# Splitting the weights inside the first pass, and a product moved from DVE to Pool

## The chip, the cores and the metric

One core of a Trainium2 chip (trn2) runs the whole program in one launch. Time is device time in microseconds. Engines: TensorE (PE, with its weight loads PEld), VectorE (DVE), ScalarE (ACT), GpSimd (POOL), SyncE (SP, here only an issuer of DMAs). Each has its own instruction queue, in order; they wait for each other by semaphores.

## The reference

x is (16, 512, 256) in float32. Two layers with residuals: an attention-like mixer, then a mixture of experts. Cut to what matters:

```python
# mixer, on LN(x)
xx = shift of the first 64 channels forward, of the next 64 back by one token
xk, xv, xr = x*mix + xx*(1 - mix)            # one mix per k, v, r
k, v, r = xk @ Wk.T, xv @ Wv.T, xr @ Wr.T
# scan over tokens, per channel, ew = exp(decay/T), u = first/T
out = (a + exp(u + k)*v) / (b + exp(u + k))
a, b = a*ew + exp(k)*v, b*ew + exp(k)
x1 = x + LN((sigmoid(r) * out) @ Wo.T)
# mixture of experts, on LN(x1): 8 experts, the best 2 by softmax(logits)
y = sum over the 2 of gate_e * expert_e(x1n) + shared(x1n)    # each silu(w1 x)*(w3 x) @ w2
out = x1 + LN(y)
```

## The kernel before

Every float32 matrix product is made of three products of parts: each operand is a `hi` (rounded by ACT) plus a `lo` (operand minus hi, by DVE or POOL), and PE adds hi*hi, hi*lo, lo*hi. So the weights have to be split once, and every activation as it comes.

Three stages follow each other: `first_pass` (mixer, routing, shared expert), `expert_tiles`, `combine`. The change is in the first alone. Its sequences s = 0 to 15 of 512 tokens go through a software pipeline, written out by hand as one `body(i)` for each engine. In body i the work on k, v, r and the scans is for sequence i (`kvr`, `exps`, `scans`, `denominator`, `invert`, `gate`), that on the output projection and x1 for i-1 (`project`, `normalise_o`, `add_x`), routing and the inner part of the shared expert for i-2 (`route`, `count_tokens`, `inner`), its outer part for i-3 (`outer`, `read_y`). Bodies 3 to 15 hold all of these. The order inside a body is the order in which calls stand there, on each engine by itself; nothing reorders them.

Ahead of that, `split_weights` is a block of its own with a barrier at its end: it loads the weights, mixes them into three parts for the channels as they are (HERE), shifted (SHIFT) and the other 128 (REST), and splits all. Only then does the pass begin, and it waits for all 15 constants.

What the prediction's steps touch:
- PE, `kvr` L537, `project` L561, `count_tokens` L602, `inner` L613, `outer` L630. The second half of `outer` waits for `y_read`, since both halves use one PSUM bank.
- ACT, in body order: h_high(3), f_high(0), high_w, exps(0), f_high(1), gate_exp, exps(1), silu(0), normalise_o (tile `on`), g_high(0) (tile `g_hi`, L721), read_y(0) (L782), silu(1), normalise_x (tile `xn`), and so on to g_high(1).
- DVE: the scans b_sum L866 and a_sum L869, reciprocals L886, `gate` L894 (g = num * den), f_low L910, the copy of token numbers L940, `low_w` L1012. `low_w` makes the lo part of one sixteenth of the expert weights in each body; SP stores both parts to `w_split` for the second stage.
- POOL: `running_sums` (num L1129, den L1131), add_x L1147, g_low L1137, h_low L1153, the scales of the normalisations L50 to L55, and `send` L1161, indirect DMAs that scatter rows to the experts' slots.

## Time and profile before

| | us |
|---|---|
| median of 3 runs (1188.23 to 1189.91) | 1188.67 |
| the profiled execution | 1182.5 |
| its span | 1180.7 |
| PE busy | 1001.1 (85%) |
| DVE busy | 880.2 (75%) |
| POOL busy | 771.6 (65%) |
| ACT busy | 568.9 (48%) |

The busy share is a mean over three stages with different limits. The first 31 us have almost no PE work; from there to about 650 the first pass runs, and then the experts. The profile shows the time of each instruction and, in brackets, how long its engine sat idle before it and what ended that. Times of instructions in the steady bodies repeat from body to body to 0.1 us or so, so one body can be read as all.

### The profile page before, as it was taken

To read this page: it belongs to the slowest core of one execution; us is meant where nothing else is said; L and a number is where in the kernel's file an instruction comes from. 1 tells how busy PE (TensorE), PEld (TensorE's weight loads), DVE (VectorE), ACT (ScalarE), POOL (GpSimd) and SP (SyncE) were. 2 spreads that over 40 slices of the span, in tenths; PEclk is the share of its full clock that TensorE was granted. 3 is DMA by queue.
4 is the path that set the end of the run, shared out by engine and by line. 5 is a ranking of instruction groups with operands and counts; after the bars stand their busy time and mean duration, and the time that the engine had idled before them with its cause. 6 is when DMAs were issued, how large, how long until landed. Compare 5 with 4: busy or idle time off the path is not lost. (4 is left out here: it accounts for less than half of the span.)

```text
span 1180.7 us, 23300 instructions
## 1 busy us (share of the span) xinstructions
PE 1001.1 (85%) x6344; PEld 886.1 (75%) x6344; DVE 880.2 (75%) x2211; ACT 568.9 (48%) x1013; POOL 771.6 (65%) x790
## 2 busy tenths in 40 slices
PE   0668899999999999999997875889999999999452
PEld 0457688788878887888786764889999999999341
DVE  3588888988898889888988323656777767777486
ACT  3344564556455645564555233434444444444265
POOL 2234876787678767876786444256776667666598
PEclk9878999999999999999999777889999999999655
DMA  4233432453235323532441117679768788887797
GB/s 136 76 107 99 147 116 88 130 165 112 88 129 165 114 87 129 165 115 85 131 148 55 59 50 229 193 174 223 125 112 183 144 204 162 184 200 183 191 371 324
DMA packets 109813, 174.06 MB, mean 147 GB/s; under 512 B 13741, under 2 KB 77896, under 8 KB 109512
## 3 DMA queue, kind: packets, MB, share of 16 engines
q1 hardware_dynamic: 78568, 121.09, 31.5%
q0 software_dynamic: 26592, 35.67, 16.7%
q10 hardware_dynamic: 4608, 16.78, 3.8%
q8 instruction: 19, 0.31, 0.1%
q14 instruction: 26, 0.21, 0.1%
HBM read 173.53 MB, written 78.21 MB: 213 GB/s over the span
## 5 line engine op out<-in xcount | busy, mean ns | idle before, releaser
L1511 POOL DMA_INDIRECT sum_y<-e_y,e_row_at x142 | 224.2, 1579 | 42.8 <-issue 38.7
L1343 PE MATMUL e_h_ps<-e_z_hi,e_w 128*128 128x256 f32 x1136 | 218.9, 285 | 11.2 <-DMA e_w<-w_split 6.3
L1343 PEld LDWEIGHTS e_h_ps<-e_z_hi,e_w 128*128 128x128 f32 x1136 | 182.4, 192 | 15.0 <-issue 8.6
L1161 POOL DMA_INDIRECT slots_x<-f_xf,f_at x128 | 143.8, 1123 | 37.8 <-issue 37.8
L1343 PE MATMUL e_h_ps<-e_z_lo,e_w 128*128 128x256 f32 x568 | 160.6, 283 | 0.0
L1387 ACT ACTIVATE e_act_h<-e_h_ps,e_w 128x256 f32<-128x256 f32 x142 | 67.4, 475 | 182.9 <-PE e_h_ps L1343 167.8
L1359 PE MATMUL e_y_ps<-e_w,e_h_hi 128*128 128x256 f32 x568 | 118.3, 292 | 1.1 <-DVE e_h_lo L1433 1.1
L625 PE MATMUL f_h_ps<-f_f_hi,f_w_hi 128*128 128x512 f32 x256 | 107.5, 420 | 6.7 <-ACT f_act_h L766 3.9
L886 DVE RECIPROCAL f_den<-f_den 128x256 f32<-128x256 f32 (+1 forms) x48 | 109.2, 2278 | 0.6
L1343 PEld LDWEIGHTS e_h_ps<-e_z_lo,e_w 128*128 128x128 f32 x568 | 108.5, 191 | 0.0
L1426 DVE SCALAR_TENSOR_TENSOR e_h<-e_h_ps,e_w,e_act_h 128x256 f32<-128x256 f32 x142 | 67.3, 482 | 52.5 <-ACT e_act_h L1387 51.0
L625 PE MATMUL f_h_ps<-f_f_hi,f_w_lo 128*128 128x512 f32 x256 | 102.8, 402 | 0.0
L625 PE MATMUL f_h_ps<-f_f_lo,f_w_hi 128*128 128x512 f32 x256 | 102.6, 401 | 0.0
L919 DVE SCALAR_TENSOR_TENSOR f_h<-f_h_ps,f_bias,f_act_h 128x512 f32<-128x512 f32 x64 | 47.8, 747 | 63.0 <-ACT f_act_h L766 60.7
L1359 PEld LDWEIGHTS e_y_ps<-e_w,e_h_hi 128*128 128x128 f32 x568 | 92.2, 188 | 1.3 <-DVE e_h_lo L1433 1.3
L1129 POOL TENSOR_TENSOR f_num<-f_num,f_a_sum 128x512 f32<-128x512 f32 x32 | 41.3, 1292 | 77.1 <-DVE f_a_sum L869 76.8
L1153 POOL TENSOR_TENSOR f_h_lo<-f_h,f_h_hi 128x512 fp32r<-128x512 f32 x64 | 81.9, 1293 | 13.4 <-ACT f_h_hi L774 12.7
L1147 POOL TENSOR_TENSOR f_x<-f_on,f_x_res 128x1024 f32<-128x1024 f32 x16 | 38.8, 2424 | 73.4 <-ACT f_on L727 73.4
L34 POOL TENSOR_TENSOR e_scratch<-e_scratch 128x1 f32<-128x1 f32 x71 | 27.3, 384 | 87.2 <-DMA sum_y<-e_y,e_row_at 40.1
L766 ACT ACTIVATE f_act_h<-f_h_ps,f_bias 128x512 f32<-128x512 f32 x64 | 43.8, 685 | 82.1 <-PE f_h_ps L625 82.1
L1359 PE MATMUL e_y_ps<-e_w,e_h_lo 128*128 128x256 f32 x284 | 79.8, 281 | 0.0
L645 PE MATMUL f_shared_ps<-f_w_hi,f_h_hi 128*128 128x256 f32 x256 | 73.7, 288 | 4.8 <-POOL f_h_lo L1153 4.2
(222 smaller groups left out, 2988.9 us busy)
## 6 DMA issues: line engine op xcount, KB each, us to landing
e_w<-w_split SPq DMA_DIRECT2D x71, 514.0 KB
e_w<-w_split SPq DMA_DIRECT2D x71, 512.0 KB
...
```

The costliest lines, as they stand in the source:

```text
L625: last = pe.matmul(out[:, :], a[:, which, c, q * P:(q + 1) * P], b[p][:, c, :], start=(n == 0), stop=(n == 5))
L645: last = pe.matmul(y_ps[:, j, :], a[:, q, at:at + P], b[:, q, :], start=(n == 0), stop=(n == 3 * Q - 1))
L766: act.activation(act_h[q % 2][:, :], h1_ps[:, :], ACT.Silu, bias=bias[:, 0, q:q + 1])\
L886: dve.reciprocal(den[c][:, at], den[c][:, at]).then_inc(rec_ready, 1)
L919: dve.scalar_tensor_tensor(out=h[q][:, :], in0=h3_ps[:, :], scalar=bias[:, 1, q:q + 1], in1=act_h[q % 2][:, :], op0=ALU.add, op1=ALU.mult) ...
L1153: pool.tensor_tensor(h_lo[:, q, :], h[q][:, :], h_hi[:, q, :].bitcast(F32), ALU.subtract)\
L1161: pool.indirect_dma_start(out=slots_x[:, :], out_offset=bass.IndirectOffsetOnAxis(ap=at[p][:, j, k:k + 1], axis=0), in_=xf[p][:, j, :], in ...
L1343: last = pe.matmul(h_ps[q][:, which, :], w13(p, q, part)[:, which, c, :], z[p % 2][:, c, :], start=(n == 0), stop=(n == 5))
L1359: last = pe.matmul(y_ps[p % 2][:, j, :], a[p % 2][:, q, j * P:(j + 1) * P], w2(p, part)[:, q, :], start=(n == 0), stop=(n == 3 * parts - 1))
L1387: act.activation(act_h[q][:, :], h_ps[q][:, 0, :], ACT.Silu, bias=bias(p, 0, q)).then_inc(silu_ready, 1)
L1426: dve.scalar_tensor_tensor(out=h[p % 2][:, q, :], in0=h_ps[q][:, 1, :], scalar=bias(p, 1, q), in1=act_h[q][:, :], op0=ALU.add, op1=ALU.mul ...
L1511: pool.indirect_dma_start(out=dst[:, :], out_offset=bass.IndirectOffsetOnAxis(ap=row_at[p][:, j:j + 1], axis=0), in_=y[p][:, j, :], in_off ...
```

## The change

Three things. (1) `split_weights` is gone as a block: its steps stand at the beginning of each engine's program in `first_pass`, in another order, with x of sequence 0 loaded before the attention weights; the buffers of the raw weights lie in rooms used later for something else; the waits for split weights are put before the first product that needs each. ACT issues three constants itself. (2) Moves inside the body: `high_w` behind f_high(1) on ACT, `low_w` from behind the moments of x to behind the aggregate of x1 on DVE, the stores of `w_split` to behind the load of x on SP, the copy of the token numbers from DVE to ACT; a small addition of one element stands in its place on DVE. (3) `gate` goes from DVE to POOL: g(0) behind add_x, g(1) between two sends.

```diff
-        split_weights(nc, attn_w, mix, ffn_w, gate_w, w_hi, w_lo, wo_hi, wo_lo, w13, w2, gw, load_ahead)
+        w_all = x1_room[:, :, :, :].rearrange("p a b n -> p (a b n)").rearrange("p (w c n) -> p w c n", w=4, c=CC)
+        w_mixed = exps_room[:, :, :].rearrange("p a n -> p (a n)")[:, 0:9 * C].rearrange("p (w a n) -> p w a n", w=3, a=3)
+        ffn_raw = h_room[:, :, :].rearrange("p a n -> p (a n)")
         @block.sync
         def _(sp):
+            sp.dma_start(mix_c, mix).then_inc(mix_in, 16)
+            sp.dma_start(x_in[0][:, :, :], by_tiles(x[0, :, :])).then_inc(x_loaded[0], 16)
+            sp.dma_start(w_all, attn_w).then_inc(w_in, 16)
+            sp.dma_start(ffn_raw, ffn_w).then_inc(ffn_in, 16)
+            sp.dma_start(gw_raw, gate_w).then_inc(ffn_in, 16)
+            sp.dma_start(x_in[1][:, :, :], by_tiles(x[1, :, :])).then_inc(x_loaded[1], 16)
...
         @block.tensor
-            pe.wait_ge(consts_in, 16 * CONSTS)
+            pe.wait_ge(first_consts_in, 16 * 3)
...
+                    if isinstance(s, int) and s == 0:
+                        pe.wait_ge(wlo_ready, (HERE, REST, SHIFT).index(part) + 1)
...
         @block.scalar
+            act.dma_start(decay_c[:, :], decay).then_inc(first_consts_in, 16)
+            act.dma_start(first_c[:, :], first).then_inc(first_consts_in, 16)
+            act.dma_start(eye[:, :], ident).then_inc(first_consts_in, 16)
...
                 normalise(LN_X1, s, p, xf[p], x1[p]).then_inc(xf_ready, 1)
+                act.activation(xf[p][:, :, C], number_s[:, bass.ds(s * SUBS, SUBS)], ACT.Copy).then_inc(numbered, 1)
...
                 f_high(i - 2, par, 0)
-                high_w(i)
                 exps(i, 0)
                 f_high(i - 2, par, 1)
+                high_w(i)
                 gate_exp(i - 2)
...
+            high_part(HERE)
+            normalise_x(0, 0)
+            high_part(REST)
+            high(0)
+            high_part(SHIFT)
+            act.activation(wo_hi[:, :, :], w_all[:, 3, :, :], ACT.Copy).then_inc(wo_hi_ready, 1)
+            act.wait_ge(ffn_in, 32)
+            act.activation(flat(w13["hi"][:, :, :, :]), ffn_raw[:, 0:W13_COLS], ACT.Copy).then_inc(ffn_hi_ready, 1)
...
         @block.vector
-                wait(dve, sent[p], landed(s - 2, p, 2 * SUBS))
-                dve.tensor_copy(xf[p][:, :, C], number_s[:, bass.ds(s * SUBS, SUBS)]).then_inc(numbered, 1)
+                dve.tensor_tensor(shift[:, 0:1], lg[:, 0, 0:1], logits_ps[:, 0, 0:1], ALU.add)
...
                 moments_x(i + 1, 1 - par)
-                low_w(i)
                 f_low(i - 2, par, 1)
...
                 invert(i, 0, slice(T // 2, T))
-                gate(i, 0, 2)
                 place(i - 2, par)
...
                 aggregate(LN_X1, i - 1, 1 - par)
+                low_w(i)
                 product(i - 2, 2)
                 denominator(i, 1)
                 low(i + 1)
                 invert(i, 1, slice(0, T))
-                gate(i, 1, 3)
...
+            moments_x(0, 0)
+            aggregate(LN_X, 0, 0)
+            dve.wait_ge(mixes_ready, 2)
+            dve.wait_ge(w_in, 16)
+            mix_part(HERE, 0, mix_c)
+            mix_part(REST, 1, both)
+            mix_part(SHIFT, 0, unmix)
+            low_part(HERE)
+            low_part(REST)
+            low(0)
+            low_part(SHIFT)
...
         @block.gpsimd
+            def gate(s, c, n):
+                pool.wait_ge(rec_ready, 3 * s + n)
+                pool.tensor_tensor(g[c][:, :], num[c][:, :], den[c][:, :], ALU.mult).then_inc(g_ready, 1)
...
                 add_x(i - 1, 1 - par)
+                gate(i, 0, 2)
                 running_sums(i, 1)
...
                 g_low(i, 0)
-                send(i - 2, par, 0, (2, 3))
+                send(i - 2, par, 0, (2,))
+                gate(i, 1, 3)
                 h_low(i - 2, 2)
                 g_low(i, 1)
+                send(i - 2, par, 0, (3,))
```

How that stands in the built program. POOL, body 3, around the addition of the residual (f_x10 before, f_x1_room after), before the change:

```order
L1147 TENSOR_TENSOR f_x10<-f_on,f_x_res0 128x1024
L1129 TENSOR_TENSOR f_num1<-f_num1,f_a_sum1 128x512
L1131 TENSOR_TENSOR f_den1<-f_b_sum1,f_eku1 128x512
L50 TENSOR_TENSOR f_var20<-f_totals20,f_scale_c 128x4
L51 TENSOR_TENSOR f_minus_mean20<-f_totals20,f_scale_c 128x4
```

and after it, the same place:

```order
L1148 TENSOR_TENSOR f_x1_room<-f_on,f_x_res0 128x1024
L1132 TENSOR_TENSOR f_g0<-f_num0,f_den0 128x512
L1123 TENSOR_TENSOR f_num1<-f_num1,f_a_sum1 128x512
L1125 TENSOR_TENSOR f_den1<-f_b_sum1,f_exps_room 128x512
L50 TENSOR_TENSOR f_var20<-f_totals20,f_scale_c 128x4
```

One instruction, g0, stands between the addition and the sums of half 1. Later in the same body, on POOL after the change:

```order
L1138 TENSOR_TENSOR f_g_lo<-f_g0,f_g_hi 128x512
L1162 DMA slots_x<-f_xf1,f_at1 78336x260
L1132 TENSOR_TENSOR f_g1<-f_num1,f_den1 128x512
L1154 TENSOR_TENSOR f_h_lo<-f_h_room,f_h_hi 128x512
L1138 TENSOR_TENSOR f_g_lo<-f_g1,f_g_hi 128x512
L1162 DMA slots_x<-f_xf1,f_at1 78336x260
```

Before, both sends stood together between the first g_lo and h_lo; now g1 has taken the place of the second, which comes last. The start of ACT's queue after the change (f_exps_room holds the mixed weights, f_x_in0 is x of sequence 0):

```order
L626 ACTIVATE f_ew<-f_decay_c 128x2
L767 ACTIVATE f_w_hi<-f_exps_room 128x3x256
L680 ACTIVATE f_xn<-f_x_in0,f_offset00,f_rstd00 128x256 x4
L767 ACTIVATE f_w_hi<-f_exps_room 128x3x256
L667 ACTIVATE f_z_hi<-f_turn_ps 128x1024
L767 ACTIVATE f_w_hi<-f_exps_room 128x3x256
L774 ACTIVATE f_wo_hi<-f_x1_room 128x512
L776 ACTIVATE f_w13_hi<-f_h_room 128x2048
```

Before, all weights were copied (w13, w2, gw, w, wo) ahead of the first xn; now xn stands behind a third of one of them.

## Rows read from the trace of the kernel before

**Rows 1.** Timeline, start: start us, duration us, engine, line, instruction [idle before, releaser].
```profile
6.33 0.35 DVE L164 TENSOR_SCALAR w_mixed<-w_raw,w_mix_c 128x256 f32<-128x256 f32 x1 [3.44 <-DMA w_raw<-attn_w]
...
13.10 2.11 ACT L145 ACTIVATE f_w_hi<-w_mixed 128x2304 fp32r<-128x2304 f32 x1
...
20.88 1.40 DVE L833 BATCH_NORM_STATS2 f_stats<-f_x_in 128x6 f32<-128x256 f32 x4
...
24.65 2.07 ACT L727 ACTIVATE f_xn<-f_x_in,f_offset,f_rstd 128x256 f32<-128x256 f32 x4 [2.25 <-POOL f_offset L55]
...
26.86 1.94 PE L534 MATMUL f_turn_ps<-eye,f_xn 128*128 128x128 f32 x8 [26.86 <-ACT f_xn L727]
...
31.27 0.76 PE L556 MATMUL f_k_ps<-f_z_hi,f_w_hi 128*128 128x512 f32 x1 [2.46 <-DVE f_z_lo L855]
```

**Rows 2.** Timeline of PE, one steady body, and the last start of project.
```profile
335.94 0.39 PE L572 MATMUL f_turn_ps<-f_wo_hi,f_g_hi 128*128 128x256 f32 x1 [1.29 <-POOL f_g_lo L1137]
...
347.85 0.29 PE L609 MATMUL f_shared_ps<-f_mask,f_tri 128*128 128x40 f32 x1 [0.71 <-DVE f_mask L966]
...
356.96 0.28 PE L645 MATMUL f_shared_ps<-f_w_hi,f_h_hi 128*128 128x256 f32 x1
...
375.31 0.39 PE L572 MATMUL f_turn_ps<-f_wo_hi,f_g_hi 128*128 128x256 f32 x1 [1.22 <-POOL f_g_lo L1137]
...
649.61 0.58 PE L572 MATMUL f_turn_ps<-f_wo_hi,f_g_hi 128*128 128x256 f32 x1 [1.00 <-POOL f_g_lo L1137]
```

**Rows 3.** Timeline of ACT, the same body.
```profile
352.19 1.93 ACT L727 ACTIVATE f_on<-f_turn_ps,f_offset,f_rstd 128x256 f32<-128x256 f32 x4
...
354.50 0.62 ACT L782 ACTIVATE f_y<-f_shared_ps 128x512 f32<-128x512 f32 x1
...
371.83 0.58 ACT L759 ACTIVATE f_f_hi<-f_shared_ps 128x512 fp32r<-128x512 f32 x1
```

**Rows 4.** Timeline of POOL, the same body.
```profile
354.41 2.42 POOL L1147 TENSOR_TENSOR f_x<-f_on,f_x_res 128x1024 f32<-128x1024 f32 x1 [4.21 <-ACT f_on L727]
359.11 1.29 POOL L1129 TENSOR_TENSOR f_num<-f_num,f_a_sum 128x512 f32<-128x512 f32 x1 [2.28 <-DVE f_a_sum L869]
...
370.20 1.25 POOL L1161 DMA_INDIRECT slots_x<-f_xf,f_at  x1 [0.17 <-issue]
...
373.99 1.26 POOL L1137 TENSOR_TENSOR f_g_lo<-f_g,f_g_hi 128x512 fp32r<-128x512 f32 x1
```

**Rows 5.** Timeline of DVE, the same body.
```profile
356.07 1.84 DVE L866 TENSOR_TENSOR_SCAN f_b_sum<-f_ew,f_ek 128x512 f32<-128x512 f32 x1
...
372.44 0.69 DVE L910 TENSOR_TENSOR f_f_lo<-f_shared_ps,f_f_hi 128x512 fp32r<-128x512 f32 x1 [1.19 <-ACT f_f_hi L759]
...
374.48 2.84 DVE L1012 TENSOR_TENSOR f_w_raw<-f_w_raw,f_w_high 128x768 fp32r<-128x768 f32 x1
```

**Rows 6.** Timelines of DVE and POOL, places where they meet or don't.
```profile
68.35 0.96 DVE L1012 TENSOR_TENSOR f_w_raw<-f_w_raw,f_w_high 128x768 fp32r<-128x768 f32 x1 [0.54 <-ACT f_w_high L699]
...
77.47 1.34 POOL L53 TENSOR_TENSOR f_rstd<-f_var,f_scale_c 128x4 f32<-128x4 f32 x1
...
79.46 1.01 POOL L53 TENSOR_TENSOR f_rstd<-f_var,f_scale_c 128x4 f32<-128x4 f32 x1
...
643.03 1.88 DVE L894 TENSOR_TENSOR f_g<-f_num,f_den 128x512 f32<-128x512 f32 x1
643.10 1.25 POOL L1137 TENSOR_TENSOR f_g_lo<-f_g,f_g_hi 128x512 fp32r<-128x512 f32 x1
```

**Rows 7.** Timeline of PE, bodies 1 and 2.
```profile
86.42 1.97 PE L534 MATMUL f_turn_ps<-eye,f_xn 128*128 128x128 f32 x8 [7.57 <-ACT f_xn L727]
...
92.25 0.77 PE L556 MATMUL f_k_ps<-f_z_hi,f_w_hi 128*128 128x512 f32 x1 [3.85 <-issue]
```

**Rows 8.** Timeline of PE, body 0, behind a hole.
```profile
42.21 0.76 PE L556 MATMUL f_k_ps<-f_z_hi,f_w_hi 128*128 128x512 f32 x1 [2.68 <-DVE f_num L864]
...
45.34 0.41 PE L556 MATMUL f_r_ps<-f_z_lo,f_w_hi 128*128 128x512 f32 x1
```

More of the change, by code:

```diff
@@ L294, in first_pass @@
         g_lo = sb("g_lo", [P, CC, T], F32R)
-        x1 = [sb(f"x1{p}", [P, SUBS, C]) for p in range(2)]
+        x1_room = sb("x1_room", [P, 2, SUBS, C])
+        x1 = [x1_room[:, p, :, :] for p in range(2)]
         xf = [sb(f"xf{p}", [P, SUBS, ROW]) for p in range(2)]
@@ L324, in first_pass @@
         warm = sb("warm", [P, 2])
+        W13_COLS, FFN_COLS = 2 * CC * Q * P, 3 * CC * Q * P
+        w_all = x1_room[:, :, :, :].rearrange("p a b n -> p (a b n)").rearrange("p (w c n) -> p w c n", w=4, c=CC)
+        w_mixed = exps_room[:, :, :].rearrange("p a n -> p (a n)")[:, 0:9 * C].rearrange("p (w a n) -> p w a n", w=3, a=3)
+        ffn_raw = h_room[:, :, :].rearrange("p a n -> p (a n)")
+        gw_raw = lg[:, 0:CC, :]
+        mix_c, unmix, both = (best[:, n, 0:3 * CC].rearrange("p (w c) -> p w c", w=3) for n in range(3))
+        assert FFN_COLS == (Q + 2) * T and W13_COLS + Q * C == FFN_COLS
         nobody = x_in[1][:, :, :].rearrange("p j c -> p (j c)")[:, SUBS * C - ROW:].rearrange("p (j c) -> p j c", c=ROW)
@@ L432, in first_pass @@
         sent = [sem(f"sent{p}") for p in range(2)]
-        CONSTS = 15
+        CONSTS = 12
         RANK_STEPS, PLACE_STEPS = 5, 6
@@ L701, in prepare @@
             def prepare(i, which, function):
-                wait(act, warmed, 2 * (i + 1) + which)
+                wait(act, warmed, 2 * i + which)
                 act.activation(warm[:, 1:2], warm[:, 0:1], function).then_inc(warmed, 1)
@@ L886, in invert @@
                 dve.reciprocal(den[c][:, at], den[c][:, at]).then_inc(rec_ready, 1)
-            def gate(s, c, n):
-                if not inside(s, SEQS):
-                    return
-                dve.wait_ge(rec_ready, 3 * s + n)
-                wait(dve, glo_ready, 2 * s + c - 1)
-                dve.tensor_tensor(g[c][:, :], num[c][:, :], den[c][:, :], ALU.mult).then_inc(g_ready, 1)
             def moments_o(s, p):
@@ L1095, in body, with mix_part, low_part @@
                     dve.tensor_copy(free_slot[:, :], count[0:1, :]).then_inc(free_ready, 1)
-            steps(dve, body, -1, *LOOP, END)
+            def mix_part(part, c, by):
+                for which in (K, V, R):
+                    last = dve.tensor_scalar(w_mixed[:, which, part, :], w_all[:, which, c, :], by[:, which, c:c + 1], None,
+                                             ALU.mult)
+                last.then_inc(mixed_ready, 1)
+            def low_part(part):
+                dve.wait_ge(whi_ready, (HERE, REST, SHIFT).index(part) + 1)
+                dve.tensor_tensor(w_lo[:, :, part, :], w_mixed[:, :, part, :], words(w_hi[:, :, part, :]), ALU.subtract)\
+                    .then_inc(wlo_ready, 1)
+            dve.wait_ge(mix_in, 16)
+            dve.tensor_scalar(unmix, mix_c, -1.0, 1.0, ALU.mult, ALU.add).then_inc(mixes_ready, 1)
+            dve.wait_ge(mixes_ready, 1)
+            dve.tensor_tensor(both, mix_c, unmix, ALU.add).then_inc(mixes_ready, 1)
+            moments_x(0, 0)
[9 more added lines that the diff above has]
+            low_part(SHIFT)
+            dve.wait_ge(first_consts_in, 16 * 3)
+            dve.tensor_scalar(u[:, :], first_c[:, :], 1.0 / T, None, ALU.mult).then_inc(u_ready, 1)
+            dve.wait_ge(wo_hi_ready, 1)
+            dve.tensor_tensor(wo_lo[:, :, :], w_all[:, 3, :, :], words(wo_hi[:, :, :]), ALU.subtract).then_inc(wo_lo_ready, 1)
+            dve.wait_ge(ffn_hi_ready, 1)
+            dve.tensor_tensor(flat(w13["lo"][:, :, :, :]), ffn_raw[:, 0:W13_COLS], words(flat(w13["hi"][:, :, :, :])),
+                              ALU.subtract).then_inc(w13_lo_ready, 1)
+            dve.wait_ge(consts_in, 16 * CONSTS)
+            dve.tensor_copy(tri_s[:, :], tri_in)
+            dve.tensor_copy(ones_s[:, :], ones_in)
+            dve.wait_ge(ew_ready, 1)
+            steps(dve, body, 0, *LOOP, END)
             tile_slots_out()
```

199 lines of the change are left out of this document (79 added, 120 removed).

## The prediction

> **What bounds the kernel now.** I read four views of the profile before the change, in this order: the timeline of the first 32 us, the timeline of one steady body of the first pass engine by engine, the waits of the PE in it, and the rows in which DVE and POOL run side by side. The second half (expert tiles, combine) isn't edited, so I treat it as shifted only.
>
> In the start stage PE has nothing to do until 31.27 us, when the first product for k begins [rows 1]. The weights have arrived at 6.33 (DVE's first multiplication), but the moments of the first sequence are taken only at 20.88, behind the whole split and a barrier. From there a chain without a hole runs: moments, scales, the normalised xn at 24.65, its transposes at 26.86, z_hi, z_lo, PE.
>
> Then come 16 bodies. I count a body from the first matmul of `project` (L572) to the next one. Bodies 3 to 15, 13 of them, have all parts at work. The last starts of `project` are 649.61 and, eight bodies before, 335.94: 39.2 us each [rows 2]. The one from 335.94 to 375.31 (39.37) is my pattern. PE waits in it in only two places: 0.71 for the mask before `count_tokens`, and 1.22 for g_lo before `project`. So PE is nearly the bound, at most 1.9 us a body can be won, and 13 x 1.93 = 25 us in all. But a cycle through the other engines has the same length: `project`, kvr, `inner(0)`, ACT's `on` at 352.19, POOL's add_x at 354.41 (18.47 after the body's start), num at 359.11, a send at 370.20, g_lo at 373.99, `project` [rows 2 to 4]. In its second part POOL has no slack except the hole between the end of add_x (356.83) and num (359.11), where it waits for two scans of DVE [rows 4, 5].
>
> What matters for the change: a DVE instruction with two operands in SBUF stands still while a POOL instruction runs. The b_sum scan at 356.07 took 1.84 us and ended 1.08 after add_x did; a_sum follows it, and num comes 2.28 after add_x's end. The subtraction of the expert weights (`low_w`) took 0.96 with POOL idle and 2.84 beside two POOL instructions [rows 4 to 6]. So DVE's time is less full than it looks, and work given to POOL comes back to DVE as standstill.
>
> **The start: what goes.** The kernel no longer has the separate block. x of sequence 0 is loaded second, half a megabyte ahead of the attention weights. The weights (1 MB) are there at 6.33 [rows 1], queue and latency included, so half as much ahead of them costs at most 3.1 and I take 1.9: they land at 8.2. DVE multiplies the first third (three instructions of 0.35, overlapping) to 9.1; ACT copies it (768 of the 2304 columns that took 2.11, so 0.7, with hand-overs 0.9) to 10.0 and then normalises. The scales of x are ready by then: x, ahead of the weights, lands at some 5.5, and rows 1 give 3.8 us from moments to xn, so 9.3. xn starts at 10.0, 14.65 earlier than at 24.65. Between xn and z_hi ACT does another third of 0.7, while PE transposes (hidden); before z_lo DVE does two subtractions of 0.96 (the same 768 columns) [rows 6], the second of which needs that third (it ends at 14.1; z_hi is there at 15.2, so hidden). From xn to the first product there were 6.62 us; the same holds, and it starts at 16.6. The split of the shared-expert weights (2048 columns on DVE, 2.6 by the 0.96 for 768) now lies behind z_lo, beside PE's first products for k, v and r; if it weren't hidden it would cost up to 2.6. The start at 31.27 becomes 16.6: gain 14.7 us, bounds 12 (weights at 10, the split late) to 16.5 (weights at 6.4).
>
> **The fill.** Body 0: g is made on POOL (1.27 for a POOL instruction of 128x512, as in rows 4), longer than on DVE, while DVE saves its part; `low_w` now stands before the denominator of half 1. Both signs, +0.4 (bounds -0.7 and +1.3). Body 1: ACT's queue is `on`, g_hi(0), then the next xn. g(0) stands on POOL behind add_x, so g_hi, formerly ready at once, waits for 2.42 + 1.27 and a hand-over of 0.3: 4.0. The transposes at 86.42 had PE waiting 7.57 us for that xn [rows 7]; they move to 90.4. From transposes to first product is 31.27 - 26.86 = 4.4, so the product at 92.25 moves to 94.8: +2.6 (bounds 0 and 4). Body 2 has no wait for the mask to win, but has the price of g(0) before the scan, 1.27, and of `low_w`, 0.7: +2.0.
>
> **A steady body.**
> 1. The mask. `low_w` (2.84) leaves the place before the second f_lo and the copy of the numbers goes to ACT as one small instruction: the mask is ready over 2 us sooner, the 0.71 wait goes, add_x starts at 17.76 after the body's start instead of 18.47. What is late next is DVE's denominator, which needs POOL's den, one send later than now; DVE then reaches the b_sum scan about when it does now, while add_x runs.
> 2. g(0) on POOL. add_x ends at 20.1, g(0) at 21.4. The b_sum scan is issued at about 19 and waits for both; the 2.28 of both scans follow, num starts at 23.7 instead of 23.17: +0.5. (1.27 paid, 0.71 won.)
> 3. g_hi(0) on ACT waits for g(0). Queued behind it: `read_y(0)`, silu(1), the next xn; PE waits for the first two. g_hi and `read_y` (0.62 at 354.50, rows 3) are 0.6 each: done at 22.6. PE's `outer(1)` needs it: it started at 356.96 (21.02) and would start at 20.2, now at 22.65, a new PE wait of 2.4. From there PE needed 17.1 to the end of its work before `project` (idle from 374.09): 39.8. So even a perfect POOL leaves a body of 39.4 to 39.8, no shorter than today.
> 4. `low_w` after the moments of x1. DVE issues it just before POOL's den ends; POOL then has four instructions of 4 columns for the scales with gaps. In rows 6, at 77.47, such a scale took 1.34 beside a DVE instruction with two operands, and 1.01 at 79.46 with none: a DVE instruction half beside it held POOL 0.33. `low_w` is 0.96 long, so POOL is held 0 to 0.9; I take 0.7.
> 5. One send before the last g_lo becomes g(1): a saving of some 0.3, as the send at 370.20 took 1.25 beside DVE's product and there are 3.8 us from it to g_lo; one send, g, h_lo are 0.96 + 1.27 + 1.25 = 3.5.
> Steps 2, 4 and 5: g_lo is 0.9 later, `project` at 40.2. A second way: the send before g(1), at 34.26 now, starts 1.2 later, so g(1) ends at 35.5 + 1.1 + 1.27 = 37.9, and ACT's g_hi(1) and h_hi stand ahead of f_hi(0) (0.6 each), then f_hi 0.58, DVE's f_lo 0.69, PE's four transposes some 0.4: 40.8. I take 40.4 against 39.37, **+1.0 a body, 13.0 in all**, bounds +0.1 (step 3 alone) and +1.9 (below).
>
> **The end of the pass.** In body 16 g(1), which took DVE 1.88 us beside POOL (643.03 to 644.91, rows 6), stands on POOL behind g_lo (to 644.35) and a send of 1.1: it ends at 646.8, f_hi is 1.9 later, of which PE's wait of 1.00 for g_lo at 649.61 hides half: +0.8.
>
> Sum: -14.7 + 0.4 + 2.6 + 2.0 + 0.8 = -8.9, and +13.0, gives **+4.1 us**. The profiled execution took 1182.5 (span 1180.7), so 1186.6; the three timed runs have a median of 1188.67, 6.2 more, and the forecast for that is 1192.8. The rivals' times below are on the same footing.
>
> **A rule to weigh.** In rows 6 DVE's g started at 643.03, before POOL's g_lo at 643.10, and yet it ended at 644.91, 0.56 after g_lo (644.35). So I let POOL's next instruction, g(0), go ahead of the waiting scan. The Trainium skill (page "SBUF — State Buffer", section "Who interferes with whom") says that a DVE instruction with two SBUF inputs contends with a GpSimd one that reads SBUF, and that the one issued first gets the shared pair for its whole length; by that the scan, waiting since 19, would go first. The trace bears out the standstill, not this order. It is rival 3.
>
> **Rivals.**
> 1. Not slower: `low_w` doesn't hold POOL, because the small instructions leave no opening and the sends behind them don't mind. It speaks for it that DVE lost every such meeting in rows 5 and 6 but one; against it that one, the 1.34. A body is then +0.3, body 2 +1.3: -9.6 + 3.9 = -5.7, **1183.0**.
> 2. Both PE waits go and nothing comes instead: 13 x -1.93 = -25, and the fill and the end cost nothing: with the start -39.7, **1149**. It would need read_y not to stand behind g_hi(0), which the order of ACT denies.
> 3. The scan takes its turn between add_x and g(0): g(0) ends 1.1 later, and PE's way (39.4 to 39.8) becomes 40.8, +1.4 a body: -8.9 + 18.2 = +9.3, **1198.0**.
> 4. The clock: PE's new hole of 2.4 us is followed by matmuls at half speed. After a hole of 2.68 the matmul at 42.21 lasts 0.76, against 0.41 at 45.34 [rows 8]: 3.1 us at half speed, some 1.6 lost; holes of 1.3 in the steady body did nothing. PE's way becomes 41.3, +1.9 a body: -8.9 + 24.7 = +15.8, **1204.5**. Decides from a hole somewhere between 1.3 and 2.68.
>
> **How the numbers follow.** Forecast 0.38, own range 1188 to 1197; rival 1 0.27 (1179 to 1187); rival 2 0.06; rival 3 0.13; rival 4 0.15; the rest for surprises of either sign. A difference under 0.2% (2.4 us, 1186.3 to 1191.0) can't be told from none. Faster: rival 2, most of rival 1 and a tail of the forecast where the start gains 16.5: 0.35. Same: 0.16. Slower: 0.49. The range for 8 in 10 is 1179 to 1205; it leaves out rival 2 and the tails.
>
> **What would show it.** First product on k_ps near 16.6 us instead of 31.27. PE's wait before `count_tokens` gone, and a new one of 2.4 before the second `outer` of each body, put down to ACT's y. POOL's g right behind add_x, a b_sum scan (half 1) of some 3.5 us. g_hi(0) waiting for POOL. Bodies of 40.4 between `project` starts. I am wrong if bodies are under 39.4 (then step 3 failed), or if the first product comes later than 20.

## The result: slower, 1246.7 us against 1189.3

The changed kernel takes 1246.73 us (median, 1245.57 to 1247.77), the kernel before beside it 1189.29 us: a ratio of 1.048, 95% interval 1.046 to 1.050. The profiled execution took 1247.77 with a span of 1245.6, 64.9 more than before, and the clock granted to TensorE is 0.896 on average, formerly 0.928. The medians below leave out two executions far above the others of their kernel (2488.6 us in e9, 1351.6 us in e10).

The start did what it should. In the timeline of PE after the change, the first product for k begins 14.68 us sooner than in [rows 1]:

```profile
16.59 0.76 PE L500 MATMUL f_k_ps<-f_z_hi,f_w_hi 128*128 128x512 f32 x1 [2.42 <-issue]
...
75.85 1.97 PE L476 MATMUL f_turn_ps<-eye,f_xn 128*128 128x128 f32 x8 [11.89 <-ACT f_xn L680]
...
352.35 0.36 PE L517 MATMUL f_turn_ps<-f_wo_hi,f_g_hi 128*128 128x256 f32 x1
...
363.69 0.29 PE L556 MATMUL f_shared_ps<-f_mask,f_tri 128*128 128x40 f32 x1 [0.15 <-DVE f_mask L923]
...
376.00 0.58 PE L595 MATMUL f_shared_ps<-f_w_hi,f_h_hi 128*128 128x256 f32 x1 [3.03 <-ACT f_y L736]
376.38 0.41 PE L595 MATMUL f_shared_ps<-f_w_hi,f_h_lo 128*128 128x256 f32 x1
376.59 0.41 PE L595 MATMUL f_shared_ps<-f_w_lo,f_h_hi 128*128 128x256 f32 x1
...
389.62 0.49 PE L500 MATMUL f_k_ps<-f_z_hi,f_w_hi 128*128 128x512 f32 x1 [1.30 <-DVE f_z_lo L821]
...
396.78 0.37 PE L517 MATMUL f_turn_ps<-f_wo_hi,f_g_hi 128*128 128x256 f32 x1
...
710.05 0.56 PE L517 MATMUL f_turn_ps<-f_wo_hi,f_g_hi 128*128 128x256 f32 x1
```

The third start of `project` is at 129.24, 10.27 ahead of the 139.51 before; the last is at 710.05, 60.44 behind the 649.61 of [rows 2]. So the 13 steady bodies between them have lost 70.7, 5.44 each. The body shown, from 352.35 to 396.78, takes 44.43 where [rows 2] has 39.37. Read its waits against those of [rows 2]: the mask 0.15 instead of 0.71; none for g_lo, formerly 1.22; new ones of 3.03 before the second `outer` and of 1.30 for z_lo. And behind the hole of 3.03 the matmuls of 256 columns follow each other in 0.21 with 0.41 each, where [rows 2] has 0.28: the granted clock from 376.1 to 381.2 is 0.50, the lower of its two levels, until the 24 matmuls are through at 381.29. They take 5.3 us, formerly 2.9.

Three engines explain where the holes are from. ACT, then POOL, then DVE, in the same body after the change (shown as start, duration, engine, line, instruction, and the idle time with its releaser):

```profile
374.83 0.63 ACT L674 ACTIVATE f_g_hi<-f_g 128x512 fp32r<-128x512 f32 x1 [4.88 <-POOL f_g L1132]
375.37 0.58 ACT L736 ACTIVATE f_y<-f_shared_ps 128x512 f32<-128x512 f32 x1
...
384.53 0.69 ACT L720 ACTIVATE f_h_room<-f_h_ps,f_bias 128x512 f32<-128x512 f32 x1 [1.37 <-PE f_h_ps L574]
```

On POOL:

```profile
370.25 2.41 POOL L1148 TENSOR_TENSOR f_x_room<-f_on,f_x_res 128x1024 f32<-128x1024 f32 x1 [4.21 <-ACT f_on L680]
372.61 2.19 POOL L1132 TENSOR_TENSOR f_g<-f_num,f_den 128x512 f32<-128x512 f32 x1
375.96 1.29 POOL L1123 TENSOR_TENSOR f_num<-f_num,f_a_sum 128x512 f32<-128x512 f32 x1 [1.16 <-DVE f_a_sum L835]
...
378.51 0.87 POOL L50 TENSOR_TENSOR f_var<-f_totals,f_scale_c 128x4 f32<-128x4 f32 x1
...
383.81 2.54 POOL L1154 TENSOR_TENSOR f_h_lo<-f_h_room,f_h_hi 128x512 fp32r<-128x512 f32 x2
386.29 1.30 POOL L1138 TENSOR_TENSOR f_g_lo<-f_g,f_g_hi 128x512 fp32r<-128x512 f32 x1
...
392.64 1.28 POOL L1132 TENSOR_TENSOR f_g<-f_num,f_den 128x512 f32<-128x512 f32 x1 [3.63 <-DVE f_den L852]
```

On DVE:

```profile
371.30 2.45 DVE L832 TENSOR_TENSOR_SCAN f_b_sum<-f_ew,f_exps_room 128x512 f32<-128x512 f32 x1
373.67 2.21 DVE L835 TENSOR_TENSOR_SCAN f_a_sum<-f_ew,f_ekv 128x512 f32<-128x512 f32 x1
...
378.34 0.97 DVE L969 TENSOR_TENSOR f_w_raw<-f_w_raw,f_w_high 128x768 fp32r<-128x768 f32 x1
...
385.34 0.75 DVE L877 SCALAR_TENSOR_TENSOR f_h_room<-f_h_ps,f_bias,f_h_room 128x512 f32<-128x512 f32 x1 [6.02 <-ACT f_h_room L720]
386.01 2.14 DVE L844 SCALAR_TENSOR_TENSOR f_den<-f_exps_room,f_den 128x512 f32<-128x512 f32 x1
388.07 1.21 DVE L821 TENSOR_TENSOR f_z_lo<-f_turn_ps,f_z_hi 128x1024 fp32r<-128x1024 f32 x1
```

Start with POOL's g at 372.61: 2.19 long, because the b_sum scan ran between add_x (to 372.66) and it. ACT's g_hi waits 4.88 for it, read_y stands behind g_hi, and PE's second `outer` behind read_y. With PE late, the third silu is late (384.53), DVE's third product waits 6.02, and the denominator behind it starts at 386.01. At that moment POOL has h_lo, h_lo and g_lo back to back (383.81 to 387.59). The denominator takes 0.69 alone; it stands still until POOL is through and takes 2.14. z_lo is late, hence PE's 1.30, and the reciprocal is late, hence POOL's 3.63 before the second g.

This meeting is in all 13 steady bodies, with 2.07 to 4.80 us for the denominator of half 1, and in none of those of the kernel before (0.68 each time). One body of the changed kernel shows it apart from the clock. Here the hole on PE is as long and all matmuls behind it are fast, but the denominator takes 4.80, and this body is the longest of the 13 (485.62 to 532.62, 47.00):

```profile
509.19 0.39 PE L595 MATMUL f_shared_ps<-f_w_hi,f_h_hi 128*128 128x256 f32 x1 [2.98 <-ACT f_y L736]
509.41 0.28 PE L595 MATMUL f_shared_ps<-f_w_hi,f_h_lo 128*128 128x256 f32 x1
...
516.51 4.80 DVE L844 SCALAR_TENSOR_TENSOR f_den<-f_exps_room,f_den 128x512 f32<-128x512 f32 x1
```

### The profile page after: what moved, and what is told of

Its sections match the earlier page's. It is cut to its first block and busy times, and to the rows that moved or that the text cites. A ratio compares the mean times of both kernels' runs of the same rounds, so it can differ in the third digit from the quotient of the medians.

```text
span 1245.6 us, 23249 instructions
## 1 busy us (share of the span) xinstructions
PE 1032.3 (83%) x6344; PEld 916.3 (74%) x6344; DVE 873.4 (70%) x2181; ACT 564.9 (45%) x1027; POOL 820.9 (66%) x822
## 5 line engine op out<-in xcount | busy, mean ns | idle before, releaser
L1162 POOL DMA_INDIRECT slots_x<-f_xf,f_at x128 | 135.0, 1055 | 35.4 <-issue 35.3
L595 PE MATMUL f_shared_ps<-f_w_hi,f_h_hi 128*128 128x256 f32 x256 | 86.0, 336 | 42.7 <-ACT f_y L736 38.6
L877 DVE SCALAR_TENSOR_TENSOR f_h_room<-f_h_ps,f_bias,f_h_room 128x512 f32<-128x512 f32 x64 | 46.6, 728 | 102.4 <-ACT f_h_room L720 100.2
L595 PEld LDWEIGHTS f_shared_ps<-f_w_hi,f_h_hi 128*128 128x128 f32 x256 | 60.6, 237 | 49.9 <-ACT f_y L736 44.5
L1368 PEld LDWEIGHTS e_y_ps<-e_w,e_h_hi 128*128 128x128 f32 x568 | 92.2, 188 | 1.6 <-DVE e_h_lo L1442 1.3
L1132 POOL TENSOR_TENSOR f_g<-f_num,f_den 128x512 f32<-128x512 f32 x32 | 53.5, 1673 | 57.2 <-DVE f_den L852 57.2
L1154 POOL TENSOR_TENSOR f_h_lo<-f_h_room,f_h_hi 128x512 fp32r<-128x512 f32 x64 | 81.8, 1292 | 13.6 <-ACT f_h_hi L728 12.8
L1148 POOL TENSOR_TENSOR f_x_room<-f_on,f_x_res 128x1024 f32<-128x1024 f32 x16 | 38.9, 2431 | 74.2 <-ACT f_on L680 74.2
L595 PE MATMUL f_shared_ps<-f_w_lo,f_h_hi 128*128 128x256 f32 x256 | 83.7, 327 | 0.0
L595 PE MATMUL f_shared_ps<-f_w_hi,f_h_lo 128*128 128x256 f32 x256 | 83.7, 327 | 0.0
```

The source lines that it names most:

```text
L595: last = pe.matmul(y_ps[:, j, :], a[:, q, at:at + P], b[:, q, :], start=(n == 0), stop=(n == 3 * Q - 1))
L877: dve.scalar_tensor_tensor(out=h[q][:, :], in0=h3_ps[:, :], scalar=bias[:, 1, q:q + 1], in1=act_h[q % 2][:, :], op0=ALU.add, op1=ALU.mult) ...
L1132: pool.tensor_tensor(g[c][:, :], num[c][:, :], den[c][:, :], ALU.mult).then_inc(g_ready, 1)
L1154: pool.tensor_tensor(h_lo[:, q, :], h[q][:, :], h_hi[:, q, :].bitcast(F32), ALU.subtract)\
L1162: pool.indirect_dma_start(out=slots_x[:, :], out_offset=bass.IndirectOffsetOnAxis(ap=at[p][:, j, k:k + 1], axis=0), in_=xf[p][:, j, :], in ...
L1368: last = pe.matmul(y_ps[p % 2][:, j, :], a[p % 2][:, q, j * P:(j + 1) * P], w2(p, part)[:, q, :], start=(n == 0), stop=(n == 3 * parts - 1))
```

## The experiments

Fifteen kernels, all beside runs of the kernel before (medians of 1186.1 to 1188.8 us). A body is worked out from two starts of `project` and the number of bodies between them:

| kernel | us | ratio to before (95%) | starts of `project`, bodies between | body |
|---|---|---|---|---|
| before | 1189.3 | 1 | 257.27, 649.61; 10 | 39.23 |
| changed | 1246.7 | 1.048 (1.046-1.050) | 263.50, 710.05; 10 | 44.66 |
| e1 g on DVE, both halves | 1165.9 | 0.982 (0.979-0.986) | 242.02, 590.38; 9 | 38.71 |
| e2 g of half 0 on DVE | 1192.7 | 1.005 (1.003-1.008) | 249.49, 577.20; 8 | 40.96 |
| e3 ACT's order | 1202.4 | 1.012 (1.009-1.015) | 250.66, 662.92; 10 | 41.23 |
| e4 before, with g on POOL | 1273.2 | 1.071 (1.068-1.074) | 284.40, 646.12; 8 | 45.22 |
| e5 g of half 1 on DVE | 1258.1 | 1.058 (1.054-1.062) | 268.97, 678.99; 9 | 45.56 |
| e6 ACT's order, twice | 1198.2 | 1.009 (1.006-1.012) | 250.75, 659.39; 10 | 40.86 |
| e7 hole filled | 1261.8 | 1.062 (1.059-1.066) | 266.76, 680.13; 9 | 45.93 |
| e8 e1, low_w in its old place | 1262.1 | 1.061 (1.056-1.067) | 272.42, 681.78; 9 | 45.48 |
| e9 g of half 0 ahead of add_x | 1195.6 | 1.007 (1.004-1.010) | 248.41, 576.19; 8 | 40.97 |
| e10 e9, g of half 1 on DVE | 1171.2 | 0.987 (0.982-0.993) | 241.41, 591.21; 9 | 38.87 |
| e11 denominator early | 1214.4 | 1.022 (1.018-1.026) | 256.23, 672.38; 10 | 41.62 |
| e12 e11, hole filled | 1207.7 | 1.016 (1.012-1.020) | 253.86, 669.55; 10 | 41.57 |
| e13 e8, stores early | 1186.8 | 0.999 (0.996-1.001) | 258.46, 650.78; 10 | 39.23 |
| e14 a send in POOL's run | 1231.4 | 1.038 (1.034-1.041) | 260.44, 694.00; 10 | 43.36 |
| e15 e1, f_hi first | 1165.1 | 0.980 (0.977-0.983) | 242.27, 591.26; 9 | 38.78 |

**e1: g on DVE again.**

```diff
# DVE
                 invert(i, 0, slice(T // 2, T))
+                gate(i, 0, 2)
                 place(i - 2, par)
...
                 invert(i, 1, slice(0, T))
+                gate(i, 1, 3)
# POOL
-                gate(i, 0, 2)
...
-                gate(i, 1, 3)
```

> The changed kernel with both halves of g made on DVE again, in their old places; the new start, the moved subtraction of the expert weights, the copy of the numbers on ACT, the order of the stores and the split sends stay. Theory A (all of the loss comes from g on POOL): bodies of 39.0 to 39.5 us, since the hole of 3.0 before the second `outer` and the half clock behind it go; with the start's 14.7 us this gives 1172 to 1178, under the kernel before. Theory B (the moved subtraction holds POOL for long, since its var stood 0.87 beside it, and with the copy and the stores it costs as much as g): bodies above 41, time 1200 to 1225. PE's wait before the second `outer`: none under A.

Measured: 1165.9 us, 22.9 under before, and below theory A's range as well. The spans of the profiled executions differ by 17.9: the third start of `project` (126.31) comes 13.2 sooner, the 13 bodies behind it win 7.7, 0.6 each, and what follows the last start (628.71) takes 3.0 more. All of the loss, 80.9 us, hangs on g. Theory B falls, though POOL's var takes 0.87 here too. This is faster than both kernels.

**e2 and e5: one half each.** The diff is that of e1 for half 0 alone (e2) and for half 1 alone (e5).

> The changed kernel with only g of half 0 back on DVE; g of half 1 stays on POOL. Theory A (half 0 alone does the harm, through ACT's copy of it that stands ahead of read_y): as with both on DVE, 1172 to 1182, no PE wait before the second `outer`, g of half 1 costs at most 0.5 us a body. Theory C (POOL has no slack, so each half of g costs what it takes there): half of the loss stays, bodies of 41 to 42.5, 1200 to 1215.

> The changed kernel with only g of half 1 back on DVE; g of half 0 stays on POOL behind add_x, ACT's order as in the changed kernel. With the earlier runs the two halves cost 26.8 us (half 1 alone on POOL) and 80.9 (both). Theory A (they are two mechanisms that add up: half 0 makes the hole on PE before the second `outer` and the half clock, half 1 holds up f_hi through g_hi(1)): 1166 + 54 = 1220, 1214 to 1226; the hole of 3 us and the half clock stay. Theory F (they feed each other: the denominator of half 1 meets POOL's run of three long instructions only since PE is late, and is as late here): both stay, 1235 to 1247. Theory G (half 0 alone costs little and the two only together overfill POOL): 1170 to 1195.

Measured: 1192.7 and 1258.1. Half 1 alone on POOL costs 26.8, half 0 alone 92.2, both together 80.9. They don't add up, and half 0 alone does more harm than both. None of the theories had that; e2 lies between its two ranges and e5 above all of its own. In e5 the denominator (DVE, start and duration first) takes 3.42, not 2.14: it reaches POOL's run of h_lo, h_lo and g_lo (389.31 to 393.08) earlier in it and so stands still longer. Over the 13 steady bodies it takes 3.8 on average in e5 and 2.8 in the changed kernel.

```profile
390.22 3.42 DVE L844 SCALAR_TENSOR_TENSOR f_den<-f_exps_room,f_den 128x512 f32<-128x512 f32 x1
```

What half 1 on POOL costs by itself is seen in e2, on ACT and on PE:

```profile
369.63 0.63 ACT L674 ACTIVATE f_g_hi<-f_g 128x512 fp32r<-128x512 f32 x1 [3.93 <-POOL f_g L1141]
...
370.69 0.58 ACT L713 ACTIVATE f_f_hi<-f_shared_ps 128x512 fp32r<-128x512 f32 x1
```

PE, a little later:

```profile
372.04 0.78 PE L534 MATMUL f_shared_ps<-eye,f_xf 128*128 128x128 f32 x4 [2.33 <-DVE f_f_lo L876]
```

g_hi of half 1 waits for POOL and f_hi stands behind it; PE waits 2.33 for f_lo. That is the prediction's "second way" of step 5.

**e4: the one part alone, in the kernel before.** Its diff is the reverse of e1's, with the sends split as in the change.

> The kernel before with one part of the change alone: both halves of g made on POOL, with the sends split as in the changed kernel; start, subtraction of the expert weights, copy of the numbers and stores as before. Theory A: all of the loss in the bodies is here, 5 us each, 1189 + 13 x 5 = 1254 to 1264. Theory B (the moves share in it): 1200 to 1235.

Measured: 1273.2, a little beyond theory A's span; 84 us for g on POOL, against 80.9 in the new kernel. The denominator of half 1 takes 1.33 to 4.05 in the steady bodies.

**e3 and e6: ACT's order.**

```diff
# e3 and e6
                 normalise_o(i - 1, 1 - par)
-                g_high(i, 0)
                 read_y(i - 3, 0)
                 silu(i - 2, 1)
                 normalise_x(i + 1, 1 - par)
+                g_high(i, 0)
# e6 alone; the copy of half 1 goes over the end of the body
                 f_high(i - 2, par, 0)
+                g_high(i - 1, 1)
...
-                g_high(i, 1)
```

> The changed kernel with g on POOL as it is, and only ACT's order changed: the copy of g (half 0) to g_hi comes behind read_y, the second silu and the next xn instead of ahead of them. Theory A (the hole of 3.0 us before the second `outer` and what follows from it, half clock 2.4 and the late silu, product and denominator, are the loss): the hole goes, the clock stays full, bodies of 39.5 to 40.5, and body 1 wins back up to 3: time 1178 to 1195. Theory C (POOL's load sets the body, the hole on PE is only a sign of it): the wait moves to g_lo or z_lo, bodies of 42.5 to 44.5, 1225 to 1247.

> The changed kernel with both halves of g on POOL, ACT's copy of g (half 0) behind the next xn, and ACT's copy of g (half 1) behind the first f_hi of the next body instead of ahead of it. Theory A (what the first order change left, 36 us over the version with g on DVE, is f_hi standing behind g_hi of half 1; then PE's wait of 2.4 for f_lo goes): 1170 to 1188. Theory C (POOL has too much to do in a body): the wait moves to `project` for g_lo and the time stays at 1195 to 1205.

Measured: 1202.4, nearer to theory A, whose 1195 it misses. With g still on POOL, 44 of the 81 us are back: the hole before the second `outer` is gone, and the denominator, now 29.2 after the body's start, runs ahead of POOL's run and takes 0.68. e6 wins 4 more at most, since the two intervals overlap: PE's wait for f_lo (2.44) turns into one for g_lo (2.07), as theory C had it. POOL still idles 3.69 before add_x, so it isn't full; but from num (356.45) to the end of that g_lo (373.44) it has no gap above 0.42, and this part is the next bound. PE in e6, at `project`:

```profile
373.50 0.39 PE L517 MATMUL f_turn_ps<-f_wo_hi,f_g_hi 128*128 128x256 f32 x1 [2.07 <-POOL f_g_lo L1138]
```

**e7: the hole filled, for the clock.**

```diff
+            def filler(s, p):
+                if not inside(s, SEQS) or not inside(s - 3, SEQS):
+                    return
+                pe.wait_ge(exps_ready, 6 * s + 6)
+                for n in range(12):
+                    pe.matmul(r_ps[:, :], w13["hi"][:, 0, 0, P:2 * P], f_hi[p][:, 0, :], start=(n == 0), stop=(n == 11))
...
                 inner(i - 2, par, 1)
+                filler(i, par)
                 outer(i - 3, 1)
```

> The changed kernel with 12 more matmuls of 128x512 on PE in each body of the first pass, between the second `inner` and the second `outer`, where PE stands idle for 3.0 us; they write the bank of r, which nothing reads before it is written anew, and take 12 x 0.23 = 2.8 us. Nothing else changes. Theory A (of the 5 us a body about half is the half clock behind the hole): the 24 matmuls of the second `outer` take 2.9 us again instead of 5.3, the second half's chain comes 2.4 sooner and with it z_lo and g; bodies of 40.5 to 42, time 1200 to 1220, though PE has 2.8 us more work. Theory H (the clock is only a passenger; the chain over POOL sets the length): bodies stay at 44, 1240 to 1255.

Measured: 1261.8, 15 more; my theory of the clock fell. On PE the hole is 0.21 instead of 3.03 and the second `outer` runs at full clock. But look at the end of the body:

```profile
382.19 0.39 PE L595 MATMUL f_shared_ps<-f_w_hi,f_h_hi 128*128 128x256 f32 x1 [0.21 <-ACT f_y L745]
...
395.79 0.79 PE L500 MATMUL f_k_ps<-f_z_hi,f_w_hi 128*128 128x512 f32 x1 [3.87 <-DVE f_z_lo L830]
```

And DVE in the same body:

```profile
388.94 0.75 DVE L886 SCALAR_TENSOR_TENSOR f_h_room<-f_h_ps,f_bias,f_h_room 128x512 f32<-128x512 f32 x1 [3.44 <-ACT f_h_room L729]
389.61 4.71 DVE L853 SCALAR_TENSOR_TENSOR f_den<-f_exps_room,f_den 128x512 f32<-128x512 f32 x1
```

The product comes 30.0 after the body's start (358.96) instead of 33.0, the 2.4 of clock were won. The denominator then starts 0.4 ahead of POOL's run (from 390.00) and is held for all of it: 4.71. z_lo is no sooner, PE waits 3.87 for it, and the half clock now falls on kvr behind that hole (0.79 for its first matmul). All 13 steady bodies are like that (4.70 to 4.81). So the length of the body here follows the meeting of the denominator with POOL, and filling PE's hole alone doesn't shorten it.

**e11 and e12: the denominator out of the way, without and with the filler.**

```diff
+                denominator(i, 1)
                 product(i - 2, 2)
-                denominator(i, 1)
                 low(i + 1)
```

> The changed kernel with one instruction of DVE moved: the denominator of half 1 (scalar_tensor_tensor, in place on den) ahead of the third product instead of behind it; its inputs are there 6 us before. g stays on POOL in both halves. Theory J (what sets the body is that this denominator arrives while POOL runs h_lo, h_lo, g_lo back to back and stands still until they are through, 2.14 us instead of 0.68 in the changed kernel, 4.71 with the filler, 3.42 with g of half 1 on DVE): it takes 0.7, z_lo comes 1.5 sooner and PE's wait of 1.3 for it goes; the hole before the second `outer` and the half clock behind it stay: bodies of 42.8 to 43.4, time 1224 to 1234. Theory A (the hole and the clock are all): 1244 to 1250.

> The changed kernel with both: the 12 matmuls that fill PE's hole before the second `outer`, and the denominator of half 1 ahead of the third product. Theory J with the clock (with the filler alone the 2.4 us of clock were won, and lost again to the same denominator, which then arrived where it was held for 4.7): now they are kept, bodies of 40.3 to 41.5, time 1195 to 1212, under the run with the denominator alone by some 20 to 30. If the clock is no cost in either order: within 5 us of the run with the denominator alone, or above it.

Measured: 1214.4 and 1207.7. One instruction moved wins 32 us, more than theory J's 13 to 23, with the hole and, in most bodies, the half clock still there. DVE's denominator in e11:

```profile
366.42 0.68 DVE L844 SCALAR_TENSOR_TENSOR f_den<-f_exps_room,f_den 128x512 f32<-128x512 f32 x1
```

The filler, which cost 15 before, now costs nothing: 6.7 less, where 20 to 30 were expected, and the two intervals overlap. A steady body is as long with it as without (41.57, 41.62), its 2.8 us of matmuls included; PE then waits only 1.45 in a body of e12 and is nearly the bound. What the clock costs in e11 can be read from its bodies. The one in which the whole second `outer` is slow takes 43.07, the three in which it is fast throughout (spacing 0.12) take 40.99, 40.99 and 41.63, and in the other nine a part of it is slow. So the clock is worth up to 2 us in a body there.

**e14: a pause in POOL's run.**

```diff
                 h_low(i - 2, 0)
                 h_low(i - 2, 1)
-                g_low(i, 0)
                 send(i - 2, par, 0, (2,))
+                g_low(i, 0)
                 gate(i, 1, 3)
```

> The changed kernel with one send of POOL moved: behind the two h_lo instead of behind g_lo of half 0, so that POOL's run of three long instructions is cut by the 0.17 us that a send needs before it starts. Theory J, that DVE's denominator gets in as soon as POOL pauses: it takes about 1.0 instead of 2.14, z_lo comes about 1 sooner, time 1222 to 1238. If the pause isn't long enough or a send holds DVE as the others do: the denominator takes 2 to 3 and the time stays at 1243 to 1252.

Measured: 1231.4, as theory J had it. The denominator and the send of one body, on DVE and on POOL:

```profile
382.11 0.87 DVE L844 SCALAR_TENSOR_TENSOR f_den<-f_exps_room,f_den 128x512 f32<-128x512 f32 x1
```

```profile
379.89 2.54 POOL L1154 TENSOR_TENSOR f_h_lo<-f_h_room,f_h_hi 128x512 fp32r<-128x512 f32 x2
382.59 1.25 POOL L1162 DMA_INDIRECT slots_x<-f_xf,f_at  x1 [0.16 <-issue]
```

It gets in when the h_lo end at 382.43, and is done at 382.98; the send pays 0.25. The 0.87 is not typical: in the 13 steady bodies the denominator takes 0.83 to 3.60, 2.6 on average, since it comes anywhere from just ahead of the two h_lo to their end. In this body, also of e14, it comes just ahead of them:

```profile
246.76 3.59 DVE L844 SCALAR_TENSOR_TENSOR f_den<-f_exps_room,f_den 128x512 f32<-128x512 f32 x1
```

The two h_lo of that body end at 249.79 and the denominator at 250.35, 0.56 behind them, as in the body above (0.55). So the move cuts the wait for g_lo off the end of the standstill, and no more. Whether the pause of 0.16 or the send behind it lets DVE in is not told apart: in e3 a denominator beside a send takes its 0.68, and the send 1.52 instead of 1.04.

**e9 and e10: g of half 0 ahead of add_x.**

```diff
+                gate(i, 0, 2)
                 add_x(i - 1, 1 - par)
-                gate(i, 0, 2)
```

> The changed kernel with g of half 0 on POOL ahead of add_x instead of behind it: there POOL waits 4.2 us for ACT's `on`, and the reciprocal it needs is done about 2 us before `on`. Theory A (not the work on POOL but its place cost the time): as if this half were on DVE, 1185 to 1197, no wait of ACT's g_hi(0), no hole before the second `outer`. Theory C (a POOL instruction costs its length wherever it stands, DVE's standstill included): 1215 to 1247.

> The changed kernel with g of half 0 on POOL ahead of add_x, in POOL's wait for ACT, and g of half 1 on DVE. With g of half 0 in that place and half 1 on POOL it took 1195.6, with half 0 on DVE and half 1 on POOL 1192.7, with both on DVE 1165.9. If place is all that counts for half 0: 1164 to 1170, as with both on DVE. If DVE, 0.7 us less full before `place`, hands on sooner: 1155 to 1163. If POOL pays for it: 1175 to 1190.

Measured: 1195.6, against 1192.7 with this half on DVE, and 1171.2, against 1165.9. Work that cost 54 us behind add_x costs 3 in the same engine's idle time ahead of it, where POOL waits for `on`, and these 3 are inside the two intervals. In e10 a small operation of `place` on DVE stands 1.06 beside it (0.15 in e1). The 1171.2 lies above the first bracket and under the third; its interval (0.982 to 0.993) overlaps that of e1 (0.979 to 0.986), and the bodies are alike (38.87, 38.71), so a difference to e1 isn't firmly there.

**e8 and e13: low_w in its old place, and the stores.**

```diff
# DVE, e8 and e13
                 moments_x(i + 1, 1 - par)
+                low_w(i)
                 f_low(i - 2, par, 1)
...
-                low_w(i)
# SP, e13 alone: the block that waits for w_lo_ready and stores to w_split
+                    sp.wait_ge(w_lo_ready, i + 1)
...
                 s = i - 3
                 if inside(s, SEQS):
                     store_y(s, 0)
...
-                    sp.wait_ge(w_lo_ready, i + 1)
```

> Both halves of g on DVE as in the first experiment, and the subtraction of the expert weights also back in its old place, ahead of the second f_lo; the copy of the numbers stays on ACT, the stores at the end. Against that experiment (1165.9 us): if the prediction's steps 1 and 4 stand (the move takes 2 us out of the way of the mask, 0.7 of which PE waited for, and puts 0.7 on POOL), 0 to 10 us more: 1166 to 1176. If the move is what holds POOL and costs time: 1157 to 1163.

> The run with g on DVE and low_w in its old place (1262 us), with one thing more put back: SP stores the split expert weights at the start of its body again, ahead of the stores of y and x1, so that the load of the next weights is issued about half a body sooner. If the loss of 96 us in that run is the late load (ACT's w_high waits for it, low_w for that, f_lo of half 1 stands behind low_w on DVE, PE waits 4.3 to 5.5 for f_lo): PE's wait before the routing product goes, bodies of 39 to 39.6, time 1168 to 1180, that is, the kernel before less the new start. If the place of low_w itself is bad in this kernel: above 1240 still.

Measured: 1262.1, where I had 1157 to 1176: the largest miss of the study. Follow it over four engines in e8, from SP's load to PE:

```profile
365.69 0.35 SPq L452 DMA_DIRECT2D f_w_raw<-ffn_w  x1
```

ACT's copy, which waits for that load:

```profile
369.41 0.84 ACT L652 ACTIVATE f_w_high<-f_w_raw 128x768 fp32r<-128x768 f32 x1 [3.14 <-DMA f_w_raw<-ffn_w]
```

DVE's low_w, which waits for the copy:

```profile
370.28 0.96 DVE L977 TENSOR_TENSOR f_w_raw<-f_w_raw,f_w_high 128x768 fp32r<-128x768 f32 x1 [5.41 <-ACT f_w_high L652]
```

PE's routing product, which needs the f_lo behind it:

```profile
371.89 0.38 PE L546 MATMUL f_shared_ps<-f_gw_both,f_f_hi 128*128 128x16 f32 x1 [4.33 <-DVE f_f_lo L876]
```

The stores stand at the end of SP's body, and the next load behind them. It is issued 1.3 after the body's start (364.43). The old place of low_w needs it by then; the new one, 20 us on, doesn't. In e13, with the stores early, the load is issued 5.6 ahead of the start of the body (331.38, 336.97), PE's wait there is 1.1 to 1.4, the body is 39.23 as before and 75 us are back. I had 1168 to 1180 and got 1186.8: the start's gain is lost in bodies 1 and 2. The first start of `project` is 12.2 sooner than before (57.30), body 1 takes back 3.1 and body 2 the rest: it starts at 92.30 and ends at 139.85, while before it ended at 139.51. Part of body 2 is the same meeting, with g on DVE. On DVE, then on PE:

```profile
123.72 4.89 DVE L844 SCALAR_TENSOR_TENSOR f_den<-f_exps_room,f_den 128x512 f32<-128x512 f32 x1
128.53 1.21 DVE L821 TENSOR_TENSOR f_z_lo<-f_turn_ps,f_z_hi 128x1024 fp32r<-128x1024 f32 x1
```

```profile
129.85 0.77 PE L500 MATMUL f_k_ps<-f_z_hi,f_w_hi 128*128 128x512 f32 x1 [3.72 <-issue]
```

The denominator starts 0.6 ahead of POOL's h_lo (124.31) and stands over h_lo, h_lo and g_lo (to 128.05). z_lo ends at 129.74 and PE begins 0.11 later, so what the profile calls "issue" is the wait for z_lo. What made body 2 late before that stays open.

**e15: ACT's order at the seam, on top of e1.**

```diff
-                h_high(i - 3, 3)
                 f_high(i - 2, par, 0)
+                g_high(i - 1, 1)
+                h_high(i - 3, 3)
...
-                g_high(i, 1)
```

> The version with g on DVE (1165.9 us, bodies of 38.7), and ACT's order at the seam of two bodies changed: f_hi of half 0, then g_hi of half 1, then the last h_hi, instead of g_hi, h_hi, f_hi. There PE's largest wait left is 0.4 to 0.7 for f_lo. If it goes and nothing comes instead: 13 x 0.4 = 5 less, 1159 to 1163. If g_lo, which waits for g_hi, takes its place: 1163 to 1169.

Measured: 1165.1, no different from e1: PE's wait for f_lo goes and one of 0.27 to 1.13 for g_lo comes in its place, the second of the two cases.

## Why the prediction was wrong

I forecast 1192.8 with 1179 to 1205; the time is 1246.7. The sign was that of my likeliest case, the size was not: 4.1 us more were expected, and the span grew by 64.9. The sign owes something to luck, since 4.1 was what 13.0 for the bodies left of 8.9 won elsewhere, and slower had 0.49. The start and the fill held; what failed is the price of a body, +1.0 forecast and +5.44 measured, in steps 3 and 5 and in a term that the sum didn't have.

- **The start** held: xn at 10.02 against 10.0, the first product at 16.59 against 16.6, body 1 +3.0 against +2.6, body 2 +1.6 against +2.0, and PE's wait for xn in body 1 is 11.89 at 75.85.
- **Step 1** held for the mask (0.71 to 0.15). But I took the two moves, low_w and the stores on SP, for separate edits and gave the second no price. e8 and e13 show that they hang together: the later place of low_w is what makes the later load harmless.
- **Step 2** had the right time for num (23.61 after the body's start against 23.7) by luck, with the wrong order: I let g(0) go ahead of the waiting scan. The scan went between, g(0) took 2.19, and ACT and PE got everything 1.0 later: a hole of 3.03, not 2.4. The rule of the Trainium skill that I had weighed ("SBUF — State Buffer", section "Who interferes with whom": the instruction issued first has the shared pair) was right for this scan, waiting from 371.30, and wrong for the denominator of e7 (389.61, POOL's h_lo 390.00), which was there first and lost. That was rival 3, with 0.13.
- **Step 3** failed in the sentence "From there PE needed 17.1 to the end of its work". It needed 20.8 (376.00 to 396.78): 2.4 for the clock and 1.30 for z_lo. The clock had been rival 4 at 1.6, as if it could only come alone; with the later scan it came together with rival 3. Nor does the length of the hole decide it, as that rival had it: behind holes of 2.94 to 3.04 in the changed kernel all 24 matmuls are slow in eight bodies, and behind one of 2.98 (509.19) none.
- **The term that was missing** is the denominator of half 1. I counted what stands behind read_y on ACT and on PE, and not what stands behind the late silu on DVE. Behind the third product DVE has an instruction with two operands in SBUF, and POOL at that time its longest run without a pause. e11 takes this meeting away and the body goes from 44.66 to 41.62, 3.0 of the 5.44; in the bodies read of e7, e5 and e4 it is held for 4.71, 3.42 and 4.05. Where an engine is late, it meets another part of its neighbour's schedule.
- **Step 4** held: var took 0.87 beside low_w, 0.67 more than its usual 0.20. It does so in e1 too, whose bodies are shorter than before all the same.
- **Step 5** failed: g(1) should have ended 37.9 after the body's start and ended at 41.57, since the late reciprocal kept POOL waiting 3.63. Its second way, f_hi behind g_hi(1), is real (e2: 2.33 on PE), and once it is out of the way POOL's work from num to g_lo is next (e6). So the forecast for half 1, about +1 a body with all else in order, was too low as well: 2.25 (38.71 to 40.96).
- **Rival 1** (low_w doesn't hold POOL) and **rival 2** (both waits go and nothing comes) were wrong, though the kernel without the move of g (e1) comes to 38.71.

After the last `project` the rest took 4.5 us longer (64.9 - 60.44), against 0.8 for the end of the pass; in e1 it is 3.0 more than before too (1162.8 - 628.71 against 1180.7 - 649.61). No run separates this.
